# A fused attention and expert kernel: the router's work is reordered, one weight load is held back, and fifteen products on zeros run ahead of the first keys

## The reference

```
x += xattn(layernorm(x), ctx)   # 16 heads of 32; 1601 keys per batch, one mask
x += attn(layernorm(x))         # 64 keys per batch; LoRA on queries and values
x += ffn(layernorm(x))          # h = gelu(x @ wg1 + bg1); p = softmax(h @ wg2 + bg2)
                                # the two largest of 20 p are the gates:
                                # y = sum over experts of gate_e * (x @ We_e + be_e)
```

## Time and profile before

| | |
|---|---|
| median of 3 runs | 679.64 us (677.45 to 683.41) |
| profiled execution, its own time | 681.38 us |
| its span, first to last instruction | 679.6 us |
| PE busy, share of the span | 641.8 us, 94% |
| DVE, ACT, POOL busy | 440.8, 326.8, 299.9 us |
| chain that ended last | PE 88%, DVE 4%, DMA 4%, ACT 2% |

### The profile page before, as it was taken

The page is one execution under the profiler, slowest core; times in us unless marked ns, Lnnn a source line. Parts: engine busy times, 40 slices in busy tenths (PEclk is TensorE's granted clock), DMA queues, the critical chain, the costliest instruction groups (busy, mean ns, idle before and its releaser), DMA issues.

```text
span 679.6 us, 16073 instructions
## 1 busy us (share of the span) xinstructions
PE 641.8 (94%) x6364; PEld 527.3 (78%) x6364; DVE 440.8 (65%) x999; ACT 326.8 (48%) x620; POOL 299.9 (44%) x265
## 2 busy tenths in 40 slices
PE   5999999999999999999999999999999978899980
PEld 5778878888888878888788788887788767788850
DVE  4865666666656465665654567444486685899966
ACT  4434444544444345444443345433465544899830
POOL 2215553356443553445534435312235457788320
PEclk9999999999999999999999999999999968999985
DMA  8512566544775447544655560220001798899528
GB/s 333 203 50 47 139 162 153 133 113 123 174 173 112 121 116 173 120 125 124 153 126 121 137 200 1 79 64 1 2 18 48 251 354 277 298 394 389 204 91 317
DMA packets 41817, 105.68 MB, mean 156 GB/s; under 512 B 8052, under 2 KB 8436, under 8 KB 40962
## 3 DMA queue, kind: packets, MB, share of 16 engines
q1 hardware_dynamic: 37330, 96.12, 48.2%
q0 software_dynamic: 4400, 8.41, 3.5%
HBM read 65.61 MB, written 11.34 MB: 113 GB/s over the span
## 4 chain that ended last, share of the span: by engine, by line
PE 88%; DVE 4%; DMA 4%; ACT 2%; issue 1%; another core or an unknown queue 1%; SPq 0%; POOL 0%; ACTq 0%; POOLq 0%; DVEq 0%
PE bank L195 24%; PE bank L197 23%; PE bank L196 22%; PE bank L415 5%; PE bank L397 4%; PE bank L201 3%; DMA wr<-scratch_ys 2%; PE bank L633 1%; PE bank L620 1%; PE bank L649 1%; DMA xi<-scratch_xn,row 1%; DMA craw<-in_ctx 1%; PE bank L447 1%; DVE stats L1565 0%
## 5 line engine op out<-in xcount | busy, mean ns | idle before, releaser
L1876 POOL TENSOR_SCALAR pp<-pp,rl 128x400 f32<-128x400 f32 x128 | 165.1, 1308 | 180.7 <-DVE rl L1344 180.7
L963 ACT ACTIVATE pp<-pp,acc 128x400 f32<-128x400 f32 x128 | 79.0, 619 | 66.6 <-DVE acc L1403 66.6
L1403 DVE CUSTOM_DVE_ANT_0 pp<-bank,cap 128x400 f32<-128x400 f32 x128 | 65.9, 571 | 50.9 <-PE bank L397 50.9
L195 PE MATMUL bank<-chi,wk 128*128 128x400 f32 x248 | 87.3, 352 | 0.0
L196 PE MATMUL bank<-clo,wk 128*128 128x400 f32 x248 | 85.5, 345 | 0.0
L197 PE MATMUL bank<-chi,wk 128*128 128x400 f32 x248 | 85.5, 345 | 0.0
L1395 DVE STREAM_TRANSPOSE raw<-pp 128x512 f32<-128x512 f32 x128 | 83.5, 688 | 2.2 <-POOL pp L1876 2.2
L195 PE MATMUL bank<-wv,chi 128*128 128x512 f32 x192 | 78.7, 410 | 0.0
L196 PE MATMUL bank<-wv,chi 128*128 128x512 f32 x192 | 75.4, 393 | 0.0
L197 PE MATMUL bank<-wv,clo 128*128 128x512 f32 x192 | 75.3, 392 | 0.0
L195 PE MATMUL bank<-wh,xu 128*128 128x512 f32 x144 | 59.7, 415 | 2.0 <-DVE xu L1252 1.4
(11 more groups left out here) (264 smaller groups left out, 1338.8 us busy)
## 6 DMA issues: line engine op xcount, KB each, us to landing
pt<-raw SPq DMA_DIRECT2D x256, 128.0 KB, 2.4
wr<-in_We SPq DMA_DIRECT2D x13, 1024.0 KB
craw<-in_ctx SPq DMA_DIRECT2D x15, 800.0 KB, 4.8
raw<-in_We SPq DMA_DIRECT2D x8, 1024.0 KB
acc<-in_We SPq DMA_DIRECT2D x6, 1024.0 KB
wr<-scratch_ys SPq DMA_DIRECT2D x8, 512.0 KB, 8.0
x_sb<-in_x SPq DMA_DIRECT2D x2, 1024.0 KB, 11.5
scratch_xn<-acc SPq DMA_DIRECT2D x8, 256.0 KB
```

Source lines behind the costliest of these rows:

```text
L195: pe.matmul(o, lhs[0], rhs[0], start=start, stop=False)
L963: act.activation(frame(p8), frame(p8), ACT.Exp, bias=bias, scale=-1.0, accum_out=total).then_inc(S["a_exp"], 1)
L1403: dve.tensor_tensor_reduce(out=frame(p8), in0=scores[:, p8 % 4, :], in1=cap[:, :], scale=-1.0, scalar=nm[:, b, p8:p8 + 1] if seg else 3e38 ...
L1876: pool.tensor_scalar(frame(p8), frame(p8), rl[:, n % 2, p8:p8 + 1], None, ALU.mult).then_inc(S["g_pn"], 1)
```

## The change

PE gets fifteen products of 128x128 on a zeroed part of `vv` ahead of `first_keys`; DVE zeroes that part as its first instruction. In the router the second group of four tiles is taken in two pairs, and the first pair's logits have a semaphore and a bank of their own. `placed` becomes a mask of 128 x 2 x 8 x 20 that POOL writes as soon as the experts are known (`places`), and DVE writes `put_in` from the positions and that mask, in place of the small product of line 1734. The count comes ahead of `we_lo(1)`, and PE, ACT and DVE read it before they turn or copy the first block's rows. The gates are multiplied out on DVE ahead of the blocks (one product more on DVE, two fewer on POOL), and PE and ACT turn them behind block 0. POOL makes its subtractions for the softmax after `places`. SP holds weight 7, and all behind it, until the rows of block 1 are gathered.

```diff
+            def spare(n):
+
+                pe.wait_ge(S["v_own"], 1)
+                for i in range(n):
+                    pe.matmul(pb[0][:, 0:128], vv[:, 0, 0:128], vv[:, 0, 0:128], start=True, stop=True)
+
             def opening():
+                spare(15)
                 first_keys()
...
             def opening():
+                own.on(dve.memset(vv[:, 0, 0:128], 0.0))
                 dve.memset(fl[:, 0:1], 1.0)
...
-            second_maxima(0)
-            second_maxima(1)
+            second_maxima(slice(0, 4), pb[7], 1)
+            masks(0)
+            second_maxima(slice(4, 6), pb[6], 2)
+            second_maxima(slice(6, 8), pb[5], 3)
+            masks(1)
             slots(0)
             slots(1)
...
-                dve.scalar_tensor_tensor(out=placed[:, :, t], in0=pos, scalar=128.0,
-                                         in1=place1.rearrange("p (c i) -> p c i", c=2)[:, :, t], op0=ALU.is_lt,
-                                         op1=ALU.mult).then_inc(S["v_rt"], 1)
-                chain(dve.tensor_scalar(low, pos, 127, None, ALU.bitwise_and))
+                own.on(dve.tensor_scalar(low, pos, 127, None, ALU.bitwise_and))
+                dve.wait_ge(S["g_put"], h + 1)
+                dve.scalar_tensor_tensor(out=put_in[:, :, t, :], in0=posv, scalar=128.0, in1=placed[:, :, t, :], op0=ALU.is_lt,
+                                         op1=ALU.mult)
...
-            we_lo(1)
...
+            we_lo(1)
+            dve.wait_ge(S["v_ji"], 1)
+            more = dve.value_load(count[0:1, 0:1], min_val=0, max_val=X8)
             dve.wait_ge(S["p_tab"], 2)
             dve.tensor_copy(turned_tab, pb[7][0:16, 0:128]).then_inc(S["v_rt"], 1)
...
+            dve.wait_ge(S["a_le"], 1)
+            own.on(dve.tensor_tensor(pr[:, :, :], pr[:, :, :], sel[:, :, :], ALU.mult))
+            chain(dve.reciprocal(sg[:, :], sg[:, :]))
...
-                elif n < R:
+                elif n == 6:
                     sp.wait_ge(S["d_xn"], 144)
                     sp.wait_ge(S["p_n2"], 8)
+                elif n < R:
+                    sp.wait_ge(d_xi[1], 16)
```

More of the change, by code:

```diff
@@ L136, in perceiver @@
         sel = mbd[:, :, :].rearrange("p j n -> p (j n)")[:, 0:8 * E].rearrange("p (i e) -> p i e", e=E)
-        sl2 = sb("sl2", [128, 8, E])
-        at_pos, starts = [hT[:, 320 * j:320 * j + 320].rearrange("p (c i e) -> p c i e", c=2, i=8) for j in range(2)]
+        at_pos, placed = [hT[:, 320 * j:320 * j + 320].rearrange("p (c i e) -> p c i e", c=2, i=8) for j in range(2)]
+        starts = at_pos
         si = sb("si", [128, 2, 16], u32)
-        placed = sb("placed", [128, 2, 8])
         start_of = sb("start_of", [128, 2, 8])
@@ L694, in gate_logits @@
                     for i in which:
-                        last = pe.matmul(pb[7 - i // 4][:, i % 4 * E:i % 4 * E + E], hx[:, i * 128:(i + 1) * 128], gw[:, 0:20], start=True,
+                        last = pe.matmul(pb[7 - i // 4 - i // 6][:, i % 4 * E:i % 4 * E + E], hx[:, i * 128:(i + 1) * 128], gw[:, 0:20], start=True,
                                          stop=True)
@@ L714, in finish @@
                 pe.wait_ge(S["a_gelu"], 2)
-                gate_logits(range(4, 6))
+                gate_logits(range(4, 6)).then_inc(S["p_lg"], 1)
                 pe.wait_ge(S["a_gelu"], 3)
@@ L775, in finish @@
                 last.then_inc(S["p_tab"], 1)
+                pe.wait_ge(S["v_ji"], 1)
+                more = pe.value_load(count[0:1, 0:1], min_val=0, max_val=X8)
                 turn_tokens(0)
-                pe.wait_ge(S["v_rt"], 7)
+                pe.wait_ge(S["v_rt"], 5)
                 pe.transpose(pb[0][:, 0:16], turned_tab, ident[0:16, 0:16]).then_inc(S["p_tab"], 1)
                 def turn_gates():
-                    pe.wait_ge(S["v_rt"], 8)
+                    pe.wait_ge(S["v_rt"], 6)
                     for a in range(2):
@@ L813, in finish @@
                     block_of(n)
-                    if n == 2:
+                    if n == 0:
                         turn_gates()
-                        pe.wait_ge(S["v_ji"], 1)
-                        more = pe.value_load(count[0:1, 0:1], min_val=0, max_val=X8)
                 for j in range(X8):
@@ L1231, in block_of @@
                 copy(yo[n % 4], pb[3 + n % 2][:, :]).then_inc(S["a_y"], 1)
+            act.wait_ge(S["v_ji"], 1)
+            more = act.value_load(count[0:1, 0:1], min_val=0, max_val=X8)
             turn_tokens(0)
@@ L1235, in scalar @@
                 block_of(n)
-                if n == 3:
+                if n == 0:
                     turn_gates()
-                    act.wait_ge(S["v_ji"], 1)
-                    more = act.value_load(count[0:1, 0:1], min_val=0, max_val=X8)
             for j in range(X8):
@@ L1707, in chain, with second_maxima, masks @@
                 dve.wait_ge(own.sem, own.n)
[L1709 to L1713, removed]
+            def second_maxima(t, bank, made):
+                wide, n = [128, t.stop - t.start, E], t.start % 4
+                dve.wait_ge(S["p_lg"], made)
+                chain(dve.tensor_tensor(pr[:, t, :], bank[:, n * E:(n + wide[1]) * E].rearrange("p (i e) -> p i e", e=E),
                                         bg2.unsqueeze(1).to_broadcast(wide), ALU.add))
-                for i in range(4 * h, 4 * h + 4):
+                for i in range(t.start, t.stop):
                     own.on(dve.max(out=mg[:, i, :], in_=pr[:, i, :]))
                 dve.wait_ge(own.sem, own.n)
-                for i in range(4 * h, 4 * h + 4):
+                for i in range(t.start, t.stop):
                     own.on(dve.max_index(mi[:, i, :], mg[:, i, :], pr[:, i, :]))
+            def masks(h):
+                t = slice(4 * h, 4 * h + 4)
                 dve.wait_ge(own.sem, own.n)
@@ L1779, in vector @@
             dve.tensor_copy(count[:, :], pb[1][0:1, 2 * E - 1:2 * E]).then_inc(S["v_ji"], 1)
+            we_lo(1)
+            dve.wait_ge(S["v_ji"], 1)
+            more = dve.value_load(count[0:1, 0:1], min_val=0, max_val=X8)
             dve.wait_ge(S["p_tab"], 2)
             dve.tensor_copy(turned_tab, pb[7][0:16, 0:128]).then_inc(S["v_rt"], 1)
[L1783 to L1789, removed]
+            dve.wait_ge(S["a_le"], 1)
+            own.on(dve.tensor_tensor(pr[:, :, :], pr[:, :, :], sel[:, :, :], ALU.mult))
+            chain(dve.reciprocal(sg[:, :], sg[:, :]))
+            own.on(dve.tensor_tensor(gmg[:, :, :], gmg[:, :, :], sg[:, :].unsqueeze(1).to_broadcast([128, 2, 8]), ALU.mult))
+            dve.wait_ge(S["g_gt"], 1)
+            dve.tensor_tensor(gt[:, :, 0:E], pr[:, :, :], sg[:, :].unsqueeze(2).to_broadcast([128, 8, E]),
+                              ALU.mult).then_inc(S["v_rt"], 1)
             def biases(which):
@@ L1949, in gpsimd @@
                                ALU.subtract).then_inc(S["g_rt"], 1)
[L1951 to L1962, removed]
             def load_tokens(n):
```

20 lines of the change are left out of this document (12 added, 8 removed).

## The result

The changed kernel has a median of 683.44 us (682.45 to 685.37, 22 runs), the kernel before beside it on the same chip 681.58 us (676.90 to 683.94, 22 runs). That is 1.9 us more, where 2.1 us less were forecast; the ratio is 1.0036, 95% interval 1.0021 to 1.0051. A later run of the same two kernels on another chip gave 1.0028 (1.0012 to 1.0044). Medians of different chips lie up to 4 us apart here, so only kernels that ran beside each other are compared by their times; across chips I compare ratios and stretches of the traces.

The account below looks back on a forecast made before the run. PE was taken to bound the kernel, busy 641.8 of 679.6 us, so gains lie where it stands or runs slowly. Opening 0.6 plus router and block start 1.5 gave 2.1 us: 679.64 to 677.5, range 672.8 to 681.2.

Parts of the forecast that it names:

- The spare products end at 7.3 us and the keys run at full clock: Opening: thirty records raise PE's clock near 6.0 us, so the first 24 key products take 4.41 us, not 6.89.
- Opening +0.6, between -0.3 and 1.4: Opening: PE's 1.4 us lead at line 277, partly lost on DVE's normalized tiles beside POOL; 0.6 us won.
- this collision: Opening: POOL's 2.40 us query-weight subtraction, moved to about 21.6, meets DVE's first two normalized tiles; gain -0.1 to 1.4 us.
- Table and first gather 0.3 us sooner: Router: pairs win 0.3, `put_in` on DVE loses 0.3, `row_in` wins 0.3; first gather comes at 556.0.
- Gather 2.6 us instead of 5.48: First gather, issue to landing: with weight 7 held it takes 2.6 us, rows there at 558.6, 3.1 us sooner.
- Its own small transpose, the second turn (1.1) and block 0 can start at 562.2: Start of the blocks: block 0 at 562.2, not 564.17; 2.0 us won, of which 1.5 was left in the sum.
- Block 0 costs the same 2.44: First block on PE: at half clock it takes 2.44 us, as before.
- What is won before stays won: Blocks: PE is full from 588 us and blocks follow at their products' length, so earlier gains reach the end.
- SP's hold is free: Weight 7 is issued near 559, not 552.6, and goes into idle transfer time, since ACT splits it only near 585.
- The slower one: Rival: held weight 7 crowds gathers 2 to 6 and ACT's stops; blocks 3 to 5 lose 4.2 us, 681.7; chance 0.12.
- The unnamed stops: Waits of 2.81 and 1.93 us without a named releaser, at 571 and 576 us, ahead of blocks 3 to 5.
- first rival: Blocks 3 to 5: the stops without a releaser go, PE wins 4.2 us more, total 673.3; chance 0.14.

Follow-up runs that it names:

- f4: The kernel before with only SP's hold of weight 7 added, router and opening unchanged; 680.38 us beside 680.94, ratio 1.000.
- e4: The changed kernel with the hold undone, weight 7 issued behind weight 6 again; 683.07 us, ratio 1.0044 to the kernel before.
- g1: The changed kernel with `we_lo(1)` moved back ahead of the count operations; 676.97 us beside the changed kernel's 679.53, ratio 0.998 to the kernel before.
- e1: The changed kernel without the fifteen spare products and their zeroing; 682.20 us beside 680.78, ratio 1.0017 to the kernel before.
- f1: The changed kernel with DVE's four gate operations moved behind its copies of block 0's turned rows and second table; 683.39 us beside 680.94, ratio 1.0034.
- g3: The kernel before with spare products, POOL's query-weight subtraction held and weight 7 held, router not reordered; 678.04 us beside 677.72, ratio 0.9999.
- g5: The changed kernel with `we_lo(1)` ahead of the count and POOL's query-weight subtraction held; 676.95 us beside 679.96, ratio 0.9944 to the kernel before.
- g6: The changed kernel with `we_lo(1)` ahead of the count and POOL's subtraction held, without spare products and zeroing; 677.55 us beside 679.96, ratio 0.9949.
- e2: The kernel before with only the fifteen spare products and the zeroing added; 681.04 us, ratio 1.0009.
- e3: The kernel before with the spare products, and POOL's query-weight subtraction held until two normalized tiles are written; 681.31 us, ratio 1.001.

## Why the prediction was wrong, point by point

- *The spare products end at 7.3 us and the keys run at full clock.* Right in kind; they ended at 6.33, and the first entry of the trace's clock list, at full clock, begins at 4.6 us, not 6.
- *Opening +0.6, between -0.3 and 1.4.* Wrong size, lower part of the range. The mask products moved up from 21.41 to 20.96 and not to 20.0, since DVE's reduction, which I took as fixed, itself came later with the value weight (19.62). In the second profile it came at 18.62 and they at 19.95, as forecast. The whole lead was then lost to POOL's subtraction: with it held back the stretch is 16.53 to 16.56 us, without 17.6 to 17.8. I had named this collision and taken the middle of its two outcomes. By the rule that I cited from the Trainium skill ("SBUF — State Buffer", the shared port pair) it would be -0.1; the 2.38 us of a scaling of 128x4 agree with that rule, and the changed kernel's stretch against the first profile's gives -0.07. I also compared with a kernel before whose clock rose late; against the third profile the opening lost 1.1 us.
- *Table and first gather 0.3 us sooner.* Better than forecast: 10.85 against 11.75, 0.9 us, in all profiles with the new order within 0.1.
- *Gather 2.6 us instead of 5.48.* Right in kind, 1.1 us too low: 3.68 to turned rows.
- *"Its own small transpose, the second turn (1.1) and block 0 can start at 562.2."* **This step failed.** It asks when PE, DVE and the first rows are ready and takes the second rows as there. I moved the count ahead of `we_lo(1)` and counted its 0.6 us on DVE only; POOL's queue, on which the second gather's issue comes 1.59 us behind the first one's, stood in none of my terms. That 0.4 us shift of `we_lo(1)` put its start right at the issue's. The issue grew by 2.6 us, the second turning came 3.97 us and not 1.27 behind the first, and block 0 began 20.8 us behind the first logits' sum by the chain, in which I had counted. That is where it was before (20.8), and I had 18.9 (562.2 - 543.34). With the one call moved back it is 19.1.
- *Block 0 costs the same 2.44.* It took 3.41 in both profiles of the changed kernel, and 1.36 and 1.00 against 0.91 for its last four products: 1.0 to 1.4 us more than in the profile that I had. But the row that I counted from was itself chance, since the third profile of the kernel before had the long block 0 too. The granted clock was at half for 20.5 us in the changed profile, 17.1 in its second, 17.1 in all three of before and 13.7 with `we_lo(1)` moved back.
- *"What is won before stays won."* Not borne out. f4 starts block 0 1.8 us sooner and has a ratio of 1.000. From block 0's start to the last scatter's issue the profiles take between 88.4 and 93.6 us, more of a spread than anything that was won ahead of it.
- *SP's hold is free.* Borne out by e4 and f4, though weight 7 was issued at 565.81, 19.7 us behind the first logits' sum and not 15.7: the hold waits for the second rows, and these were late.
- *The rivals.* None of them was it. The slower one had the held weight as its cause, and e4, without the hold, is no faster. The unnamed stops of the first profile are no property of the order: they came in two of three executions of the kernel before. The range's lower end, 672.8, was called half of the first rival; it is the bound for 1% faster and lies under that rival's full 673.3.

The sum as measured in the traces against the first profile: router 0.9 sooner, first gather 1.85 sooner, second rows 2.7 later, block 0 1.0 to 1.4 longer, opening 0.1 later: 1.0 to 1.5 us slower. Against the third profile of before little but the opening is left, 1.1 us. The medians say 1.8 to 1.9, the ratios 1.9 to 2.4. So two things have to be kept apart. That the gain of 2 us at block 0 was missing is the second gather's issue, and g1 shows that the one call is worth 2.56 us, more than the whole loss. Where the changed kernel loses 1.9 us against the kernel before isn't shown, since block 0 starts equally late in both. Stops of ACT in blocks 2 to 4 come and go between executions of both kernels by up to 4 us (109.70 to 113.92 us from the logits' sum to the last scatter's issue in the changed order, e1 and f1 among them; 110.49 to 112.66 in the kernel before), and single profiles can't weigh them. For the same reason it is open why g3 and f4 gain nothing in the median while g5 and g6, whose traces are 1 us better there, gain 3.

## What to carry to other kernels

When you move work on one engine, write down what every other queue is doing at the new start, not only who waits for the result: the work here moved by 0.4 us on DVE and cost 2.6 us on POOL, though no semaphore ties the two. Where two engines can lock each other out, place the long work so that the short, urgent instruction comes first, or hold the long one by a wait; and price a collision that you can name at what its rows show in full, not at the middle. Before you count a gain against one profile, learn from a second one what in it is chance.

## What the runs showed of the hardware that was not expected

- **How long a gather's issue takes beside DVE's subtractions of two operands goes with where it begins.** Begun 0.02 to 0.03 us behind the start of a run of four 128x512 subtractions: 3.76, 3.76, 3.77 and 3.34 us (changed kernel twice, e4, f1; with e1 3.77). Begun 0.42 to 0.43 us behind it: 1.13 or 1.14 (before three times, e2, e3, f4, g1, g3, g5, g6). With none beside it: 1.00. Where it is locked out it ends 0.9 us behind the run's end in f1, about its own microsecond, which fits a wait for the whole run of four instructions. The Trainium skill ("SBUF — State Buffer", section on the two separate sides) states that whichever of the two starts first holds the pair "for the whole instruction", and that GpSimd can't write its descriptors while VectorE runs an operation in a two-port mode. The 3.3 to 3.8 us are like that, though with subtractions of two tensors and over four instructions rather than one; the 1.13 us begun in the middle of such an instruction don't follow from it. I have no run that tells why.
- **The lock works on the smallest instruction:** 128x4 on DVE, 0.22 us alone, took 2.38 us 0.03 us behind the start of POOL's 2.39 us.
- **A drop of the clock in some executions only.** In the cross attention, near 410 us, PE runs for 3.4 us at half clock in some profiles while it is fully busy. The windows of the changed kernel's two profiles there (us, busy time of five engines, granted clock, DMA share, GB/s), the first:

```profile
411.00:413.00 2.00, 2.00 (x6) 1.61 (x5) 1.36 (x3) 1.53 (x3) 0.61 (x2) 0.50 0.00 0
```

and the second:

```profile
411.00:413.00 2.00, 2.00 (x15) 1.75 (x14) 1.68 (x4) 1.19 (x3) 0.00 (x0) 1.00 0.00 0
```

  From the queries to the first logits' sum the six profiles with it take 514.8 to 515.7 us, the twelve others 513.2 to 514.0. It stands in 6 of the 18 profiles: the changed kernel's first, e3, f3, f4, g5 and g6, and not in its second nor in the three of the kernel before. f4 has nothing of the reordered router and no spare products, so neither is needed for it. What brings it on is open.
